# A recurrent scan, its preparation and a distance table: three pieces of work put in another place

## The reference, cut to what matters

```python
xz = x @ W_in.T; u, z = split(xz)
u = silu(causal_conv(u, conv_w, 4 taps) + conv_b)
dt, B, C = split(u @ W_x.T)
delta = softplus(dt @ W_dt.T + b_dt)
for t in range(L):
    h = exp(delta[t] * A) * h + (delta[t] * u[t]) * B[t]
    y[t] = sum over the state of h * C[t]
y = (y + u * D) * silu(z); out = y @ W_out.T
```

```python
D = sqrt(max(aa + bb - 2 * a @ b.T, 0))      # 32 x 257 distances of a sequence
R[i, j] = D[i, j] + min(R[i-1, j], R[i, j-1], R[i-1, j-1])
walk back from the last cell; add up the rows met into each token
```

## Time and profile before

| | us |
|---|---|
| median of 3 runs (lowest, highest) | 1948.91 (1948.72, 1953.33) |
| the profiled execution: time | 1953.92 |
| the profiled execution: span | 1952.1 |
| TensorE busy in the span | 1711.4 (88%) |
| VectorE | 1011.8 (52%) |
| ScalarE | 761.7 (39%) |
| GpSimd | 703.1 (36%) |

### The profile page before, as it was taken

One profiled execution on the slowest core, in us unless ns is written; L12 is line 12 of the kernel. 1 busy time (PEld: TensorE's weight loads), 2 busy tenths in 40 slices (PEclk: granted clock), 3 DMA queues, 4 the chain that ended last, 5 costly groups with the idle time before them and its releaser, 6 DMA issues.

```text
span 1952.1 us, 24426 instructions
## 1 busy us (share of the span) xinstructions
PE 1711.4 (88%) x9096; PEld 821.3 (42%) x9096; DVE 1011.8 (52%) x1520; ACT 761.7 (39%) x1201; POOL 703.1 (36%) x430
## 2 busy tenths in 40 slices
PE   7888886898999999999997759999812979899998
PEld 4666663542322332332333525444401557644443
DVE  2444444255888888888884333222359464522121
ACT  1333332196676666666661222111413240112121
POOL 0433330215998998998995010000000014000000
PEclk8999997798999999999999768999865879789999
DMA  2111101002000100100100600111062100101110
GB/s 68 32 32 32 32 27 52 0 8 96 12 12 7 29 12 7 29 12 7 29 6 17 223 1 0 33 48 32 5 143 70 33 0 1 44 1 43 44 43 21
DMA packets 36491, 65.63 MB, mean 34 GB/s; under 512 B 13509, under 2 KB 22617, under 8 KB 34981
## 3 DMA queue, kind: packets, MB, share of 16 engines
q1 hardware_dynamic: 33204, 63.42, 11.0%
q10 hardware_dynamic: 3200, 1.07, 0.2%
HBM read 55.80 MB, written 8.67 MB: 33 GB/s over the span
## 4 chain that ended last, share of the span: by engine, by line
PE 80%; DVE 12%; ACT 2%; DMA 2%; issue 2%; POOL 1%; SPq 1%; DVEq 0%; ACTq 0%; POOLq 0%
PE ps L845 17%; PE ps L888 7%; PE ps L1376 6%; PE ps L2123 6%; PE ps L2112 6%; PE ps L860 5%; PE ps L201 4%; PE ps L1389 3%; PE ps L342 3%; PE ps L347 3%; PE ps L224 3%; PE ps L360 2%; DVE arena L477 2%; PE ps L1887 2%; PE ps L1903 2%
## 5 line engine op out<-in xcount | busy, mean ns | idle before, releaser
L1156 POOL TENSOR_TENSOR arena<-arena 128x768 f32<-128x768 f32 x248 | 521.5, 2122 | 75.2 <-DVE arena L1106 45.0
L845 PE MATMUL ps<-arena 32*128 32x512 f32 x2016 | 368.7, 647 | 2.9 <-DMA arena<-m_bd 2.9
L1106 DVE TENSOR_TENSOR arena<-arena,ps 128x1024 f32<-128x1024 f32 x248 | 302.0, 1218 | 11.7 <-POOL arena L1156 5.5
L845 PEld LDWEIGHTS ps<-arena 32*128 32x128 f32 x2016 | 130.0, 184 | 194.2 <-issue 165.2
L1086 DVE TENSOR_TENSOR arena<-arena,ps 128x1024 f32<-128x1024 f32 x124 | 151.4, 1221 | 87.5 <-PE ps L845 87.5
L1012 ACT ACTIVATE arena<-arena 128x1024 f32<-128x1024 f32 x124 | 131.0, 1057 | 166.1 <-DVE arena L1086 166.1
L2069 POOL TENSOR_TENSOR arena<-arena 128x1024 f32<-128x1024 f32 x16 | 29.9, 1896 | 435.0 <-DVE arena L2002 421.7
L888 PE MATMUL ps<-arena 128*32 128x512 f32 (+15 forms) x1024 | 136.2, 604 | 9.4 <-DVE arena L1106 8.9
L1019 ACT ACTIVATE arena<-ps 128x1024 f32<-128x1024 f32 x124 | 127.0, 1024 | 19.7 <-PE ps L845 3.4
L1021 ACT ACTIVATE arena<-arena 128x1024 f32<-128x1024 f32 x124 | 131.1, 1057 | 3.9
L1376 PE MATMUL ps<-arena 128*128 128x512 f32 x288 | 131.8, 602 | 0.6 <-ACT arena L1441 0.6
(11 more groups left out here) (291 smaller groups left out, 2345.3 us busy)
## 6 DMA issues: line engine op xcount, KB each, us to landing
arena<-ctxT SPq DMA_DIRECT2D x32, 257.0 KB, 3.0
arena<-ctxT SPq DMA_DIRECT2D x8, 1028.0 KB, 15.2
arena<-L_ffn_w SPq DMA_DIRECT2D x16, 512.0 KB, 4.3
arena<-ctx_rows SPq DMA_DIRECT2D x8, 960.0 KB
m_rows<-arena SPq DMA_DIRECT2D x16, 256.0 KB, 3.0
arena<-m_rows SPq DMA_DIRECT2D x64, 64.0 KB
arena<-L_ffn_eW SPq DMA_DIRECT2D x8, 512.0 KB, 3.5
m_yd<-arena SPq DMA_DIRECT2D x64, 32.0 KB, 2.3
```

The costliest lines, as they stand in the source:

```text
L845: mm = nc.tensor.matmul(ps[:, bank + jj, :], weights[r], m_row[r, n // CH % 2, n % CH, :], start=start, stop=True)
L1106: nc.vector.tensor_tensor(m_h[:, u, n % 2], m_xa[:, u, n % 2], ps[:, bank:bank + 2, :], ALU.add).then_inc(S["m_use"], 1)
L1156: nc.gpsimd.tensor_tensor(x, x, m_h[:, u, (n - 1) % 2].rearrange("p j d -> p (j d)")[:, own], ALU.mult).then_inc(S["m_kept"], 1)
```

## The change

It does four things. (1) In the scan `read_out(n - 1)` is queued behind `drive(n, 1)`, where it was queued behind `drive(n, 0)`. (2) The convolution of the second half of the tokens is done by VectorE into the place of its result, with one product and three fused multiply-adds per block, and ScalarE's Silu reads it there; Relu of the step sizes goes from ScalarE to VectorE (as a maximum with 0), and before Abs ScalarE waits for it. (3) The queues of the preparation are put in another order: TensorE does both halves' projections, then all step sizes, then u by token, C and B in other banks, z behind them; ScalarE interleaves the Silus of both halves and the two halves' squares. The semaphores' lists follow. (4) `dist` has the token as its first axis and the three segments of a token side by side: a store is 128 pieces of 1044 B, where it was 384 of 348 B; a load is pieces of 348 B, 32 per partition, where it was one of 11136 B.

```diff
 
-        dist = nc.dram_tensor("dist", (3, T, 87), F32, kind="Internal").ap()
+        dist = nc.dram_tensor("dist", (T, 3, 87), F32, kind="Internal").ap()
 
...
                     pe.wait_ge(*S.at("mi_ev_d", g + 1))
-                    if g == 6:
-                        pe.wait_ge(*S.at("m_eaev", 1))
-                    if g == 7:
-                        pe.wait_ge(*S.at("m_alev", 1))
                     x3 = half(m_xm, c, h).rearrange("p (b t) -> p b t", t=L)
...
                 pe.wait_ge(*S.at("ld_m", dma_n["ld_m"]))
-                pe.wait_ge(*S.at("mc_ev_a", IC * h + IC))
+                pe.wait_ge(*S.at("mc_ev_a", 2 * IC - 1 + h))
                 product(IC * h, P, [(m_wx[:, k, 0:P], half(m_u, k, h)) for k in range(IC)], "m_dtmm")
...
                     q = 4 * h + i
-                    pe.wait_ge(*S.at("md_ev", 2 * q + 2))
+                    pe.wait_ge(*S.at("md_ev", q + 1))
+                    pe.wait_ge(*S.at("md_pos", q + 1))
+                    if h and i < 2:
+                        pe.wait_ge(*S.at("m_cev", 2 * i + 2))
+                    if h and i == 2:
+                        pe.wait_ge(*S.at("m_bev", 2))
                     for c in range(IC):
...
             mm.then_inc(S["m_alt"], 1)
+            steps_and_b(1)
             step_sizes(0)
-            conv(1)
+            pe.wait_ge(*S.at("m_alev", 1))
+            pe.wait_ge(*S.at("m_eaev", 1))
+            step_sizes(1)
             u_by_token(0)
-            steps_and_b(1)
-            step_sizes(1)
             for h in range(NH):
-                pe.wait_ge(*S.at("m_dudone", h + 1))
-                spread_c(h, bank_of(0, h))
-            pe.wait_ge(*S.at("m_dudone", 3))
+                pe.wait_ge(*S.at("md_ev", 5 + h))
+                pe.wait_ge(*S.at("md_pos", 5 + h))
+                spread_c(h, bank_of(1, h))
+            pe.wait_ge(*S.at("md_ev", 7))
+            pe.wait_ge(*S.at("md_pos", 7))
             pe.wait_ge(*S.at("m_dtev", 4))
-            for h in range(NH):
-                for q in range(4 * h, 4 * h + 4):
-                    mm = nc.tensor.transpose(ps[:, bank_of(0, 2), q * NS:(q + 1) * NS], m_Bc[NS:P, q * P:(q + 1) * P],
-                                             ident[NS:P, NS:P])
-                mm.then_inc(S["m_bmm"], 1)
+            for q in range(TT):
+                mm = nc.tensor.transpose(ps[:, bank_of(1, 2), q * NS:(q + 1) * NS], m_Bc[NS:P, q * P:(q + 1) * P],
+                                         ident[NS:P, NS:P])
+            mm.then_inc(S["m_bmm"], 1)
             u_by_token(1)
             for n in range(8):
-                if n == 0:
-                    pe.wait_ge(*S.at("m_dudone", 4))
-                elif n < 3:
-                    pe.wait_ge(*S.at("m_cev", 2 * n))
-                elif n == 3:
-                    pe.wait_ge(*S.at("m_bev", 2))
+                if n < 4:
+                    pe.wait_ge(*S.at("m_dudone", n + 1))
                 else:
                     pe.wait_ge(*S.at("mz_ev", n - 3))
-                product(bank_of(0, (n + 3) % 4), P, [(m_win[:, k, (IC + n % 4) * P:(IC + n % 4 + 1) * P], half(U[2], k, n // 4))
-                                                     for k in range(DC)], "mz_mm")
+                product(bank_of(0, n % 4), P, [(m_win[:, k, (IC + n % 4) * P:(IC + n % 4 + 1) * P], half(U[2], k, n // 4))
+                                               for k in range(DC)], "mz_mm")
             pe.wait_ge(*S.at("mz_ev", 8))
...
                 drive(n, 0)
-                if n:
-                    read_out(n - 1)
                 if rated(n + 2):
...
                 drive(n, 1)
+                if n:
+                    read_out(n - 1)
                 if rated(n + 2):
...
                 g = IC * h + c
-                act.wait_ge(*S.at("mc_mm", g + 1))
-                nc.scalar.activation(half(m_u, c, h), ps[:, g, :], ACT.Silu,
+                if h == 0:
+                    act.wait_ge(*S.at("mc_mm", c + 1))
+                    src = ps[:, g, :]
+                else:
+                    act.wait_ge(*S.at("m_dconv", c + 1))
+                    src = half(m_u, c, h)
+                nc.scalar.activation(half(m_u, c, h), src, ACT.Silu,
                                      bias=m_cb1[:, c:c + 1]).then_inc(S["mc_ev_a"], 1)
...
                     q = 4 * h + i
-                    act.wait_ge(*S.at("md_mm", q + 1))
-                    nc.scalar.activation(m_delta[:, q, :], ps[:, bank_of(h, i), :], ACT.Relu).then_inc(S["md_ev"], 1)
+                    act.wait_ge(*S.at("md_pos", q + 1))
                     nc.scalar.activation(m_e[:, q, :], ps[:, bank_of(h, i), :], ACT.Abs).then_inc(S["md_ev"], 1)
-                act.wait_ge(*S.at("md_ev", 8 * h + 8))
+
+            def exponential(h):
+                act.wait_ge(*S.at("md_ev", 4 * h + 4))
                 nc.scalar.activation(m_e[:, 4 * h:4 * h + 4], m_e[:, 4 * h:4 * h + 4], ACT.Exp, scale=-1.0).then_inc(S["m_e"], 1)
...
                                    .rearrange("p (j t s) -> p j t s", t=L, s=SEQS)[:, :, :, s],
-                                   ps[r, bank_of(0, h), :].rearrange("p (j s t) -> p j s t", s=SEQS, t=L)[:, :, s, :]).then_inc(S["m_cev"], 1)
+                                   ps[r, bank_of(1, h), :].rearrange("p (j s t) -> p j s t", s=SEQS, t=L)[:, :, s, :]).then_inc(S["m_cev"], 1)
 
             def b_by_token(h):
-                act.wait_ge(*S.at("m_bmm", 2))
+                act.wait_ge(*S.at("m_bmm", 1))
                 nc.scalar.copy(m_Btok[:, 4 * h:4 * h + 4].rearrange("p q n -> p (q n)"),
-                               ps[:, bank_of(0, 2), 4 * h * NS:4 * (h + 1) * NS]).then_inc(S["m_bev"], 1)
+                               ps[:, bank_of(1, 2), 4 * h * NS:4 * (h + 1) * NS]).then_inc(S["m_bev"], 1)
 
...
                 convolved(0, c)
+                convolved(1, c)
             steps_and_b(0)
...
             nc.scalar.copy(m_EA, ps[:, 6, :]).then_inc(S["m_eaev"], 1)
+            steps_and_b(1)
             parts(0)
+            exponential(0)
             square(0, 0)
             square(0, 1)
-            convolved(1, 0)
+            parts(1)
             square(0, 2)
-            for c in range(1, IC):
-                convolved(1, c)
             square(0, 3)
+            exponential(1)
             square(0, 4)
-            steps_and_b(1)
-            parts(1)
             square(1, 0)
+            spread_c(0)
             square(1, 1)
-            spread_c(0)
-            square(1, 2)
             spread_c(1)
...
             b_by_token(1)
+            square(1, 2)
             square(1, 3)
...
                     act.wait_ge(*S.at("mz_mm", 4 * h + i + 1))
-                    nc.scalar.activation(half(m_z, i, h), ps[:, bank_of(0, (i + 3) % 4), :], ACT.Silu).then_inc(S["mz_ev"], 1)
+                    nc.scalar.activation(half(m_z, i, h), ps[:, bank_of(0, i), :], ACT.Silu).then_inc(S["mz_ev"], 1)
             logged(1)
...
                 nc.vector.tensor_copy(half(m_xm, g % IC, g // IC), ps[:, g, :]).then_inc(S["mi_ev_d"], 1)
+            dve.wait_ge(*S.at("ld_m0", dma_n["ld_m0"]))
+            for c in range(IC):
+                dve.wait_ge(*S.at("mi_ev_d", IC + c + 1))
+                x3, y3 = (half(v, c, 1).rearrange("p (b t) -> p b t", t=L) for v in (m_xm, m_u))
+                ch.link(nc.vector.tensor_scalar(half(m_u, c, 1), half(m_xm, c, 1), m_cw[:, c, KW - 1:KW], None, ALU.mult))
+                for s in range(1, KW):
+                    ins = nc.vector.scalar_tensor_tensor(out=y3[:, :, s:], in0=x3[:, :, :L - s],
+                                                         scalar=m_cw[:, c, KW - 1 - s:KW - s], in1=y3[:, :, s:],
+                                                         op0=ALU.mult, op1=ALU.add)
+                    if s < KW - 1:
+                        ch.link(ins)
+                ins.then_inc(S["m_dconv"], 1)
             two = view(CONST + 1856, SEQS)
...
             nc.vector.tensor_copy(m_al[2], m_left).then_inc(S["m_alev"], 1)
+            for q in range(TT):
+                dve.wait_ge(*S.at("md_mm", q + 1))
+                nc.vector.tensor_scalar(m_delta[:, q, :], ps[:, bank_of(q // 4, q % 4), :], 0.0, None,
+                                        ALU.max).then_inc(S["md_pos"], 1)
             for h in range(NH):
...
                 pool.wait_ge(*S.at("m_quad", 5 * h + 5))
-                pool.wait_ge(*S.at("md_ev", 8 * h + 8))
+                pool.wait_ge(*S.at("md_pos", 4 * h + 4))
                 for q in range(4 * h, 4 * h + 4):
...
                     r = slice(B * k + SL * g, B * k + SL * g + SL)
-                    sp.dma_start(d_D[r, k:k + L].rearrange("p j i -> p (j i)"),
-                                 dist[k, g * P:(g + 1) * P].rearrange("(b j) i -> b (j i)", j=L)).then_inc(S["d_back"], 16)
+                    sp.dma_start(d_D[r, k:k + L],
+                                 dist[g * P:(g + 1) * P, k].rearrange("(b j) i -> b j i", j=L)).then_inc(S["d_back"], 16)
```

(7 more changed lines are left out.)

## The result

The changed kernel takes **2004.9 us** (median of 4 runs, 2000.9 to 2007.7) against 1948.9 of before (4 runs, 1948.7 to 1953.3): ratio **1.028**, 95% interval 1.0256 to 1.0305, or +54.6 us (+50 to +59) by the ratio; the two medians are 56.0 apart. The forecast was 2001, 1971 to 2014, slower with 0.83. The profiled execution of after is one of 2006.54 us; the forecast for the profiled one was 2006.

What follows compares the result with a forecast made beforehand. The scan's step was bound by a 4.56 us ring from VectorE's state through read-out and rates; moving the read-out lengthens another ring to 5.04. +52 - 0.3 + 0 = +52 gives 2001 us for the median, range 1971 to 2014.

Steps and rivals of the forecast that it cites:

- part 1: Scan, read-out queued behind the drive of unit 1: step from 4.56 to 5.04 us, together +52 us.
- Loop B: Scan ring through PSUM banks: L1019, drive of unit 1, logs, their spread; 4.07 us, slack 0.49, 5.04 with the read-out.
- the give-back at a change of group: Scan, between groups of 32 steps: about 1.3 us given back each time, -5.2 in all.
- my ring: Scan: exponential L1019, drive of unit 1, the moved read-out, logs, their spread; forecast 5.04 us a step.
- (a): Rival, scan: read-out runs beside drive or logs, POOL bounds at 4.21 a step, -41 us, 1908; chance 0.12.
- (b): Rival, scan: the read-out costs the ring just about its slack, 4.56 a step again, 1948 us; chance 0.05.
- (c): Rival, distances: forecast's recurrence, but reads spread over 16 engines, end near 1430 instead of 1440.2, 1991 us; chance 0.10.
- (d): Rival, preparation: VectorE's convolution late, over 3.3 us a block, +5 at most, 2006 us; chance 0.03.
- Part 2: Preparation, second half's convolution on VectorE and new order: 13 us of TensorE were cover, not path; -0.3 us, -3 to +3.
- Part 3: Distances by token: reads stay on four engines, 0.025 us a piece, writes 0.047, sum 21.8; 0 us, -4.5 to +4.
- the stall: Distances before the change: reads 18.3 and writes 3.5 us on each of four DMA engines, 21.8 us.
- L1772's wait: Sign, distances: the wait of L1772 for the distances would still be about 15 us.

Runs made afterwards that it cites:

- e1: The kernel before with only the read-out moved behind the drive of unit 1: 2003.3 us, ratio 1.0269.
- e9: The kernel before with only the change's preparation (convolution of the second half on VectorE and its queue order): 1948.9 us, ratio 0.9979.
- e8: The kernel before with the new layout of the distances and 6 wide loads in place of 24: 1949.3 us, ratio 0.9983.
- e7: The kernel before with 6 wide loads of the distances in place of 24, old layout: 1947.2 us, ratio 0.9984.
- e3: The kernel before with only the new layout of the distances, its store and its 24 loads: 1960.3 us, ratio 1.0058.
- e5: The kernel before with the read-out moved behind the drive of unit 1 and only 256 of its 512 columns computed: 1951.3 us, ratio 1.0000.
- e6: The kernel before with the read-out in its old place and only 256 of its 512 columns computed: 1918.3 us, ratio 0.9829.
- e4: The kernel before with the read-out put between the rates and the drive of unit 1: 1970.7 us, ratio 1.0117.
- e10: The kernel before with a third state buffer and the read-out, in its old place, of the step before last: 1944.0 us, ratio 0.9949.
- e12: The kernel before with the read-out moved behind the drive of unit 1 and taken from a third state buffer, one step later: 2003.8 us, ratio 1.0283.

## Why the prediction was right, point by point

**The bound and the sum of part 1** held. Loop B with the read-out was put at 5.04, measured 5.06: read-out to logs 0.99 for 0.97, drive to read-out 1.06 as taken, the other terms to 0.01. Thirty such intervals in four groups are 60 us; the give-back at a change of group was 1.10 for the 1.3 taken; 60 - 4.4 = 55.6 stands against the +54.4 of e1's scan, and e1's time is +52.4. In the whole change the scan is only 47.9 longer, since the new preparation alone makes it 5.5 shorter (e9: 584.8 for 590.3). By the Trainium skill, TensorEngine Tiling (Array Packing), Key Properties, a change of the tiling mode drains the array. The prediction set 0.06 a step for that, a number that no row gives. Drive to read-out is 1.06 here, the same as drive to logs before, which changes the mode too (32-row to 64-row tiles). So whatever a drain costs is alike in both, and no run here shows its size; the measured excess over my ring is 0.02 a step.

**Rivals.** (a) needed a read-out that costs loop B under 0.49; it costs 0.99. (b) likewise. (c), reads over 16 engines, is refuted by the completions, four to a load. e8, whose reads have sixteen, is the nearest to what it would have given: 29.6 us in the stage for 38.9, about the 10 us of (c), though with fewer loads. By the Trainium skill, DMA: Bandwidth & Descriptors, Why a DMA increments its semaphore by 16 and not by 1, a DMA uses the largest number of engines up to 16 that divides the slowest dimension of both sides. The traces agree: 4 partitions and 4 completions in after, 16 partitions and 16 completions in e7. (d): VectorE's convolution of a block takes 2.66 us (2.3 forecast), well under 3.3, and is hidden, as its rows of after show:

```profile
373.87 0.47 DVE L1058 TENSOR_SCALAR arena<-arena 128x512 f32<-128x512 f32 x1
374.38 2.23 DVE L1060 SCALAR_TENSOR_TENSOR arena<-arena 128x496 f32<-128x496 f32 x3
376.52 0.48 DVE L1058 TENSOR_SCALAR arena<-arena 128x512 f32<-128x512 f32 x1
```

**Part 2.** "-0.3, bounds -3 to +3". The stretch up to the scan is 0.8 shorter. In after, against the earlier trace rows:

```profile
402.07 1.92 ACT L954 ACTIVATE arena<-arena 128x2048 f32<-128x2048 f32 x1
...
425.53 11.59 DVE L1090 SCALAR_TENSOR_TENSOR arena<-arena 128x2048 f32<-128x2048 f32 x5
...
435.81 1.33 ACT L980 ACTIVATE arena<-arena 128x512 f32<-128x512 f32 x2
```

With the 1.8 us lead taken out, the exponential is at 403.9 (404.1 forecast), VectorE's run of quadratics at 427.3 (427.7), and the logarithm at 437.6 (438.1, before 438.38). The step that failed is the bracket at its end, "the first steps at half clock as now": they were not at half clock. TensorE's granted clock in the first two stretches of 5 us of the scan (the column after the busy times), of before:

```profile
453.20:458.20 5.00, 5.00 (x22) 1.68 (x22) 2.21 (x2) 3.71 (x4) 0.00 (x0) 0.67 0.99 330
458.20:463.20 5.00, 5.00 (x20) 1.30 (x18) 3.01 (x4) 2.11 (x2) 3.30 (x2) 0.50 0.36 139
```

and of e9, the preparation alone:

```profile
450.40:455.40 5.00, 4.28 (x24) 1.52 (x26) 3.04 (x3) 4.26 (x5) 0.56 (x1) 1.00 1.01 341
455.40:460.40 5.00, 5.00 (x38) 1.38 (x36) 3.81 (x5) 3.71 (x4) 4.19 (x3) 1.00 0.34 127
```

In before the clock falls to 0.50 of full (1.2 of 2.4 GHz), in e9 it stays at full. The first read-out starts 10.4 us after the scan in before and 7.4 in e9; with the read-out moved 13.7 in e1 and 9.6 in after. That is 3 to 4 us, which with the 0.8 would make e9's 4. About 1 of it is not the clock: in e3, where the old preparation kept full clock, the first read-out starts at 8.4. It is no accident of one run: the first 5 us were at 0.66 to 0.71 in eight of ten profiles with the old preparation and at 1.00 in all four with the new one. But of those eight only four (before, e1, e5, e6) were at 0.50 in the second 5 us as well; the others (e4, e8, e10, e12) were back at 0.95 to 1.00, and in e8 the first read-out starts at 8.2, no later than in e3. So the clock's 2 to 3 us fall due in some executions of the old preparation and not in others. How often, the profiles do not say, and that e9's 4 us in the medians are made of this is likely, not shown.

**Part 3.** "0, bounds -4.5 to +4" was mis-sized and is the largest error: about +6 in the stage, +11 in the time of e3. The 5 between them have no place of their own in the trace; in e3's profile the stretches beside the stage are longer too, by no more than they scatter. The step that failed is the piece of 348 B read, taken at 0.025 between 0.021 and 0.029. It took 0.036, so a load engine's work is 27.9 us and not the 24 x 32 x 0.025 = 19.2. The stores were near (9.0% of 16 x 39 us over 1024 pieces is 0.055, for 0.047). My bound came from other traffic with smaller pieces; a longer one was open. The sum was also set against the wrong stretch: 21.8 us was called the stall, but from the last store to the first step it is 18.4, since reads begin before that store. One of the signs failed with it: L1772's wait of "still about 15" is 20.0.

The two misses, -4 and +6 to +11, partly cancel in the sum: 2001 forecast and 2004.9 measured is closer than the parts were, and that much of it is luck.

## What to carry to other kernels

Before moving an instruction off a wait, write down every ring that runs through the queue it is moved in, its length and its slack: here the wait removed was real, but the ring on the other side had 0.49 us of slack for a 0.99 us instruction. Then add up the engine's list from one step to the next, since that is the floor once rings are gone. For DMA, count partitions of the destination first, and the size of pieces second: with six loads of 16 partitions the layout made no difference (30.0 and 29.6 us).

## What the runs showed of the hardware that was not expected

- The price of a small piece was not fixed: 348 B read from DRAM took 0.036 us in after on four engines, but in e8, where 16 engines worked at once, the 3072 pieces took 171 us by the packets' own times (37.4% of 16 x 28.6 us, from 1403 to 1431.6), 0.056 each. The wide loads were quicker all the same, since the work was spread.
- Issuing a load took SyncE 0.30 us (median of 24 in before, 4 pieces each), 0.42 in e7 (16 pieces) and 0.63 in e8 (512 pieces). In after, with 128 pieces each on four engines, it took 0.60 to 1.96, with 0.93 on average for the last 14 (13.0 us), where each of the four engines had 1.15 us (32 x 0.036) of work for a load. So the number of pieces alone does not set it. That the queue pushes back at the rate of the engines is the likely reading of what lies above 0.60; it was not tried by itself.
- A preparation with less TensorE work ahead of the scan (13.27 us of convolution gone) left the clock at full when the scan began, in all four profiles. TensorE's idle time just ahead of the first drive does not decide it: 2.9 us in before and 2.8 in e9; and e3 and e8, with the old preparation and 1.1 and 1.4 us, began at 1.00 and 0.66. What decides was not tried.
